# Attention with normed queries and keys: token-major heads replaced by feature-major heads, and its first pair's preparation moved into the last mixture pair

## The reference, cut to what matters

```python
x = x + _L0_ffn_ref(_layernorm(x), ...)                    # mixture of 8 experts, top 2
x = x + _L1_xattn_ref(_layernorm(x), ctx_1024, _lenS2, ...)  # the attention of this document

def _L1_xattn_ref(q, kv, x_seqlens, Wq, Wk, Wv, Wo, q_norm_w, k_norm_w):   # 16 heads of 64
    def rms_norm(x, w):
        return x * jax.lax.rsqrt(jnp.mean(jnp.square(x), -1, keepdims=True) + 1e-5) * w
    qh = rms_norm(heads(q @ Wq), q_norm_w)
    kh = rms_norm(heads(kv @ Wk), k_norm_w)
    vh = heads(kv @ Wv)
    scores = jnp.where(mask, einsum('bhld,bhsd->bhls', qh, kh) / 8, -1e9)
    return einsum('bhls,bhsd->bhld', softmax(scores), vh) @ Wo
```

## Time and profile before

| what | us |
|---|---|
| median of 3 runs | 1215.52 (1208.99 to 1219.18) |
| the profiled execution | 1212.19 |
| its span in the trace | 1210.4 |
| PE busy | 1013.4 |
| DVE busy | 857.5 |
| ACT busy | 573.5 |
| POOL busy | 221.5 |

### The profile page before, as it was taken

The page is one execution under the profiler, slowest core; times in us unless marked ns, Lnnn a source line. Parts: engine busy times, 40 slices in busy tenths (PEclk is TensorE's granted clock), DMA queues, the critical chain, the costliest instruction groups (busy, mean ns, idle before and its releaser), DMA issues.

```text
span 1210.4 us, 32163 instructions
## 1 busy us (share of the span) xinstructions
PE 1013.4 (84%) x11942; PEld 802.7 (66%) x11942; DVE 857.5 (71%) x1921; ACT 573.5 (47%) x1102; POOL 221.5 (18%) x243
## 2 busy tenths in 40 slices
PE   5679999888888887899899999899998673698757
PEld 5448888556656666778678877677877552376535
DVE  5576776789999996555677676677677387576647
ACT  1224443657666663343555565546665231344324
POOL 4563221101111101331100000000000122434200
PEclk9978999989999998999999999999999796599969
DMA  9200000000000000000000000000000000000001
GB/s 371 101 2 1 0 0 0 1 1 2 0 0 0 0 0 2 2 1 1 2 2 0 0 0 2 2 2 0 0 0 1 1 0 0 1 1 0 1 1 35
DMA packets 5921, 16.15 MB, mean 13 GB/s; under 512 B 729, under 2 KB 4962, under 8 KB 5218
## 3 DMA queue, kind: packets, MB, share of 16 engines
q1 hardware_dynamic: 5858, 15.29, 3.3%
HBM read 14.24 MB, written 1.05 MB: 13 GB/s over the span
## 4 chain that ended last, share of the span: by engine, by line
PE 40%; issue 22%; DVE 18%; DVEq 12%; POOL 3%; ACT 2%; POOLq 2%; PEldq 1%; PEld 1%; ACTq 0%
PE banks L1674 7%; PE banks L1747 4%; PE banks L1719 4%; PE banks L900 3%; PE banks L1136 3%; PE banks L1707 3%; DVEq L1346 2%; PE banks L1358 2%; PE banks L1735 2%; PE banks L1117 1%; DVE small L1591 1%; DVE xn L333 1%; DVEq L1012 1%; DVE xr L1011 1%; DVE small L1320 1%
## 5 line engine op out<-in xcount | busy, mean ns | idle before, releaser
L352 POOL TENSOR_TENSOR rstd<-var,nhalf 128x2 f32<-128x2 f32 x72 | 57.3, 796 | 481.2 <-DVE var L326 481.2
L1682 ACT ACTIVATE work<-banks 128x512 f32<-128x512 f32 x128 | 74.9, 600 | 70.6 <-PE banks L1674 70.6
L1339 ACT ACTIVATE work<-work 128x1024 f32<-128x1024 f32 x64 | 67.7, 1057 | 54.9 <-DVEq L1335 31.6
L1674 PE MATMUL banks<-xT_all,weights 128*128 (+1 forms) x384 | 86.2, 380 | 2.3 <-ACT work L1792 1.8
L374 ACT ACTIVATE xT_all<-banks 128x256 f32 (+1 forms) x72 | 28.3, 392 | 120.6 <-PE banks L363 119.6
L1358 PE MATMUL banks<-ident,work 128*128 128x128 f32 x512 | 68.9, 285 | 16.0 <-DVE work L1349 10.9
L929 ACT ACTIVATE work<-banks,weights 128x256 f32<-128x256 f32 x128 | 53.7, 470 | 57.7 <-PE banks L890 56.8
L1674 PEld LDWEIGHTS banks<-xT_all,weights 128*128 128x128 f32 x384 | 71.5, 190 | 13.7 <-ACT work L1792 2.6
L1826 DVE TENSOR_TENSOR work<-banks,neg_mask 128x512 f32<-128x512 f32 x64 | 40.7, 685 | 54.2 <-PE banks L1707 52.6
L1358 PEld LDWEIGHTS banks<-ident,work 128*128 128x128 f32 x512 | 60.9, 147 | 22.8 <-DVE work L1349 13.0
L1747 PEld LDWEIGHTS banks<-weights,work 128*128 128x128 f32 x512 | 58.4, 191 | 14.9 <-ACT work L1792 14.8
(11 more groups left out here) (316 smaller groups left out, 2357.8 us busy)
## 6 DMA issues: line engine op xcount, KB each, us to landing
weights<-wpack SPq DMA_DIRECT2D x1, 5381.5 KB, 32.4
weights<-wpack SPq DMA_DIRECT2D x1, 2060.0 KB, 13.5
weights<-wpack SPq DMA_DIRECT2D x1, 2049.0 KB, 17.9
weights<-wpack SPq DMA_DIRECT2D x1, 1160.5 KB, 20.1
x_all<-x_in SPq DMA_DIRECT2D x2, 512.0 KB, 4.8
ctxT_all<-ctxT_in SPq DMA_DIRECT2D x1, 1024.0 KB, 6.8
out<-x_all SPq DMA_DIRECT2D x8, 128.0 KB, 1.8
rows<-rows_in SPq DMA_DIRECT2D x1, 832.0 KB
```

The lines of the kernel that those rows point to most:

```text
L352: g.tensor_tensor(rstd, var, nhalf[:, 0:2], ALU.pow).then_inc(rstd_ready, 1)
L1339: act.activation(sm[:, u, :], sm[:, u, :], ACT.Exp, scale=scale).then_inc(h["exp"].sem, 1)
L1674: ins = pe.matmul(bank(ring.bank(f"qk{c}"))[:, j * PT:(j + 1) * PT], wt[:, 2 * (c % 4) + j, :], cols(src, p), start=True, stop=True)
L1682: act.activation(dst.rearrange("p c t -> p (c t)"), bank(ring.bank(f"qk{c}")), ACT.Copy) \
```

## The change

**The attention becomes feature-major.** `project` makes queries and keys with the weights as stationary operand, 8 units `qk0` to `qk7` of two 256-column products each, straight from `xT_all` and `ctxT_all`. ACT stores each bank plain and squares the odd ones (in the first pair all); in the bodies POOL squares the even ones from the stored tile. PE sums the squares per head (`sums`: 16 products of 128 rows x 32 columns of the array, 256 wide, in four column groups), ACT takes the inverse root of one 128x256 tile (Ln with scale and bias, Exp), PE spreads the roots times the gains back over the features (`roots_spread`, 16 products of 32 rows, 256 wide, in four row groups, into 8 banks `bc0` to `bc7`), and DVE multiplies each bank into its heads (`scaled`, 8 operations of 128x512). `mean_squares`, `divide`, `turn_qk` and the two stores of turned banks go. The next scores wait for `bc7`.

**The first pair's preparation moves.** `pro` is gone. Its units are spread among those of the mixture's last pair, which is written out behind the loop as `moe0.last`. The mixture's closing sums for its last pair (`add_up`, `ending`) move from ahead of the attention to DVE's place behind the softmax of the first body. The mixture's space in `work` and the attention's are exchanged so that both can be live; ACT's first stores of mixed heads wait for `prod_read`.

**Small things.** `make_gains` on DVE, once, after the first mixture pair. A `settle` ahead of each wait for a bank in the mixture and the attention. The barrier ahead of the attention (all banks empty) goes. POOL copies only `cs` for this attention.

```diff
-        def moe_units(nu, nd, lag):
+        def moe_units(last):
+            early, routed, late = {}, [], []
+            if last:
+                early = {1: ["gains", "qk0", "qk1"], 3: ["qk2", "qk3"], 4: ["qk4", "qk5"], 5: ["qk6", "qk7"],
+                         7: ["sums"]}
+                routed, late = [f"bc{c}" for c in range(4)], [f"bc{c}" for c in range(4, 8)] + [f"v{c}" for c in range(4)]
+            names = ["route"]
+            for j in range(8):
+                names += [f"up{j}"] + early.get(j, [])
+                if j in (3, 5, 7):
+                    names.append(f"down{j // 2 - 1}")
+            names += routed + ["combT", "down3"] + late
...
-        att1 = pipelined(scores4, mixing8, [(f"tok{u}{c}", "a") for u in range(2) for c in range(4)],
-                         values4 + [(f"turn{u}{c}", "av"[c % 2]) for u in range(2) for c in range(4)])
+        att1.pro = moe0.last
+        att1.body = stage(scores4 + queries8 + [("sums", "a")] + turned4 + scaling8[0:4] + mixed4 + scaling8[4:8]
+                          + values4, PAIRS - 1)
+        att1.epi = stage(scores4 + turned4 + mixed4, 1)
...
+            pooled = (0, 2, 4, 6)
...
+            def sums(pe, ring, i, p):
...
+                pe.wait_ge(*ring.emptied(i, "qk7"))
...
+                    pe.wait_ge(*pool_squared.at(p - 1, 1))
...
+                for m in range(4):
+                    for j in range(4):
+                        ins = pe.matmul(bk[32 * j:32 * j + 32, 0:PT], head_sum[:, m, 0, :],
+                                        squares(ring, j // 2)[:, 4 * (j % 2) + m, :], start=(m == 0), stop=(m == 3),
+                                        tile_position=(0, 32 * j))
...
+            def roots_spread(pe, ring, i, p, part):
...
+                        ins = pe.matmul(bank(ring.bank(name))[:, PT * (m % 2):PT * (m % 2) + PT],
+                                        gains_spread[32 * j:32 * j + 32, P * m:P * m + P],
+                                        head_roots[32 * j:32 * j + 32, :], start=True, stop=True,
+                                        tile_position=(32 * j, 0))
...
+                    if last:
+                        result([ring.emptied_before(i, f"o{u}1") for u in range(2)] if ring is s.body else None)
+                    if ring is s.body:
+                        sums(pe, ring, i, p + 1)
+                    probs_turned(pe, ring, i, p, 0, h["prob"])
+                    probs_turned(pe, ring, i, p, 1, h["prob"])
+                    if ring is s.body:
+                        roots_spread(pe, ring, i, p + 1, 0)
...
+                    mix(ring, i, 0)
+                    mix(ring, i, 1)
+                    if ring is s.body:
+                        roots_spread(pe, ring, i, p + 1, 1)
+                        values(pe, ring, i, p + 1)
+                        turn_normed(pe, g_of(s, p), inputs_used)
...
+            def scaled(v, ring, i, k):
+                v.wait_ge(banks_filled, ring.filled(i, f"bc{k}"))
+                v.tensor_tensor(heads_of(k), bank(ring.bank(f"bc{k}")).rearrange("p (c t) -> p c t", t=PT),
+                                heads_of(k), ALU.mult).then_inc(dve_emptied, 1)
...
+                    soft_out(v, p, 0, h)
+                    soft_out(v, p, 1, h)
+                    if last:
                         end[0](v, s, p - 1)
                         end[1](v, s, p - 1)
+                    else:
+                        prog[moe0][6][0](v)
+                        v.drain().then_inc(prod_read, 1)
+                        prog[moe0][6][1](v)
+                    if ring is s.body:
+                        for k in range(8):
+                            scaled(v, ring, i, k)
...
+            def pool(g, p):
...
+                    own = (kT if k else qT)[:, a:a + 2, :]
+                    g.wait_ge(*s.body.emptied(p, f"qk{c}"))
+                    ins = g.tensor_tensor(squares(s.body, k)[:, a:a + 2, :], own, own, ALU.mult)
```

More of the change, by code:

```diff
@@ L215, in stage @@
             return s
-        def pipelined(these, mixing, inputs, late, tail=[]):
-            s = stage([])
-            s.pro = stage(inputs + late, 1)
-            s.body = stage(these + inputs + mixing + late + tail, PAIRS - 1)
-            s.epi = stage(these + mixing + tail, 1)
-            return s
         first = stage([("none", "a")])
@@ new lines, in tensor, with part @@
+                part(s.body, 0, 0)
+                with pe.Fori(1, PAIRS - 1) as p:
+                    part(s.body, p, p)
+                pe.wait_ge(weights_in[weight_group[att1]], 16)
+                part(s.last, 0, PAIRS - 1)
+            def scalar(act):
+                def part(ring, i, p):
+                    for name in ring.names:
+                        if ring is s.last and name == "sums":
+                            act.preload_act_table_set("natural_log_exp_and_others")
+                        if ring is s.last and prog[att1][4][1](act, name):
+                            if name == "sums":
+                                store_turned(act, g_of(s, p), before(act, p))
+                            continue
+                        if not name.startswith("up"):
+                            continue
@@ L1036, in main @@
[L1036 to L1047 removed]
+                    sort(v, ring, i, p)
+                    add_up(v, p - 1)
@@ new lines, in part, with projected @@
+                        result([ring.emptied(i, f"o{u}1") for u in range(2)])
+                steps1(pe, part)
+            def projected(act, ring, i, c):
+                act.wait_ge(banks_filled, ring.filled(i, f"qk{c}"))
+                k, a = c // 4, 2 * (c % 4)
+                bk = bank(ring.bank(f"qk{c}"))
+                ins = act.activation((kT if k else qT)[:, a:a + 2, :].rearrange("p c t -> p (c t)"), bk, ACT.Copy)
+                if ring is s.pro or c not in pooled:
+                    ins = act.activation(squares(ring, k)[:, a:a + 2, :].rearrange("p c t -> p (c t)"), bk, ACT.Square)
+                ins.then_inc(act_emptied, 1)
```

762 lines of the change are left out of this document (369 added, 393 removed).

## The result

| | before | after |
|---|---|---|
| median of 9 runs, us | 1215.47 (1208.99 to 1219.18) | 1204.45 (1201.75 to 1212.92) |
| profiled execution, us | 1212.19 | 1208.06 |
| its span, us | 1210.4 | 1206.3 |

The sign is right and the time is in the range, but about half of the gain is missing. So the question is where 19.2 us became 11.

A forecast was written before the change was run, and what follows sets the result against it. DVE's own order in a chain alternating with PE was taken to bound the attention; -16.8 - 6.9 + 3.5 + 1.0 = -19.2 us gave 1193.0 from the profiled 1212.2, forecast 1195 for the median, range 1185 to 1213.

The forecast's parts named there:

- The six bodies: Normed attention's loop: period 26.7 us instead of 29.5, 16.8 us less over six passes; bounds 25.9 and 29.5.
- The three short waits: PE in a loop body, waiting for banks that DVE must free: 0.1 to 0.3 us each.
- POOL's squares: Loop bodies: POOL and DVE in each other's way add 0.4 us a period; bounds 0 and 3.3.
- the layout: One loop body laid out from its scores at 0, short waits included: ends at 26.3 us, before 0.4 for POOL.
- The last mixture pair: With `pro` in it, router to first scores takes 33.3 us instead of 40.2, 6.9 less; bounds 32.2 and 40.2.
- The first body: Attention's first body, with the mixture's closing sums on its path: 31.5 us against 28.0, 3.5 more; bounds +1.5 and +5.
- `make_gains`: Seven small DVE operations once, between the first two mixture pairs: 1.0 us more, between 0 and 2.9.
- The sum: Whole kernel: -16.8 - 6.9 + 3.5 + 1.0 = -19.2 us, 1193.0 from the profiled execution; median put at 1195.
- `epi` and all later stages keep their code, 0: Stages from `epi` on: same code, so no change in time, 0 us.
- POOL and DVE: Rival: in the attention they hold each other up or the chain stays as long; 1213.1 us, no change; chance 0.12.
- column groups without overlap: Rival: `sums` costs 7.0 us instead of 2.2 in seven bodies and the last mixture pair; 1231.4 us; chance 0.07.
- an empty last mixture pair: Rival: the last mixture pair gains nothing, its 36 units hanging on a ring of six banks; 1199.9 us; chance 0.07.

The follow-up runs named there:

- whole_after: The changed kernel run again without an edit, on another chip, for a second trace: 1205.22 us, ratio 0.9906.
- after_38_ahead: The changed kernel with 38 semaphore increments put at the head of PE's program: 1200.17 us, ratio 0.9861.

## Why the prediction was right where it was, and where it failed

- *The six bodies* (26.7 a period, -16.8): right. The steady period is 26.47, the first of the six passes takes 27.2 and the last 27.4, together 160.5 us for 176.5, so -16.0. By its own rows the forecast's six passes of 26.7 would have saved 16.3, since 176.5 is less than six times the 29.5 that the sum used. PE bounds them, as laid out. `sums` and the two spreads came at 1.94 and 2 x 1.15, for 2.2 each. The three short waits of PE are there, 0.17, 0.36 and 0.57; the last shows as issue.
- *POOL's squares* (+0.4 a period): the mechanism is right, its price on the period isn't measured. The squares don't run at 1.04 us each beside DVE but at 1.56 in the median, and in most passes one of DVE's two subtractions is held, 1.48 for 1.23, which is gone in the run without POOL's squares. That is 0.25 us of DVE's time. The steady period lies 0.17 above the 26.3 of the layout, and the run without POOL can't tell what of it is POOL's, since ACT was late in it. The forecast took DVE's loss beside POOL from `divide` at 5.03 against the softmax's operations; `pro`'s own `divide`, with nothing on POOL beside it, takes 4.63 in the trace of before, so that row said 0.4 and not 0.1. Timeline of DVE in the third pass, and POOL's durations (min/median/max):

```profile
332.60 1.23 DVE L1313 TENSOR_TENSOR work<-work,small 128x1024 f32<-128x1024 f32 x1
...
335.12 1.22 DVE L1311 TENSOR_REDUCE small<-work 128x16 f32<-128x1024 f32 x1
336.41 1.48 DVE L1313 TENSOR_TENSOR work<-work,small 128x1024 f32<-128x1024 f32 x1
```

```profile
L1693 POOL TENSOR_TENSOR weights<-work x28: 1036/1556/2024, 247.4 to 419.1; 128x512 f32<-128x512 f32 x28
...
who waited for it (us, times):
  PE banks L1448: 3.3, 1
```

  In the loop nobody waits for them; the run without them was slower. By the Trainium skill ("SBUF — State Buffer", section "SBUF: two separate sides"), among DVE's operations those with two SBUF inputs contend with a POOL operation that reads SBUF; the page names those in a two-port mode as well, which the prediction left out. The subtraction (L1313) was held, the reductions (1.20 to 1.22) were not, and the trace agrees.
- *The last mixture pair* (33.3): right, 33.67. The wait for `combT` is 0.77 where 1.1 was said, and the granted clock is 1.00.
- *The first body* (31.5): 31.68 in this trace, 30.9 to 31.0 in the other three of after. The wait of 4.20 was named; it is 2.8 in the three others, where `sums` and the transposes behind it ran slower (2.49 and 3.04 us for 1.94 and 1.97 in `whole_after`). Not named was that `sums` waits 3.32 us for POOL, because this body has no `result` to lie between; with the squares on ACT it waits 3.95 for ACT instead. It costs nothing, since PE would only have waited the longer for DVE's scaling. The total is right in this trace by two errors that cancel: the records behind the wait cost 2.4 us more than at the full clock (mix 1.99 for 1.16, spread 2.09 for 1.15, values 4.35 for 3.71), where 1.5 was added, and without that the body takes 29.3 where 30.0 was laid out.
- *`make_gains`* (+1.0): the mixture's seven pairs before the last took 119.4 us instead of 118.7, so +0.7, which is luck. The second pass, where the gains are made, is 0.6 longer than the steady ones. Each of the six passes behind the first is 0.15 longer than before, because PE waits 0.63 us for one of DVE's banks instead of 0.49; the forecast had nothing for that. And the first pass is 0.8 shorter.
- *The sum*: the changed stages gave 18.1 and 18.4 us for 19.2. The agreement at `epi` needs the 1.1 us of the first stage, which is luck. From its own sum the forecast should have said 1193.0 + 3.3 = 1196.3 for the median and not 1195.
- *"`epi` and all later stages keep their code, 0"*: this is the step that failed. The term was put at nothing because the code is the same. In the two traces of each whole kernel (before 755.7 and 762.0 us, after 770.9 and 767.1) the stages from `epi`'s scores on cost 10.1 us more after, of a gain of 19.4; the medians lose some 8. Of the 10.1, 5.6 lie in the plain attentions, where PE stops more often and where the places of the stops move with idle instructions. 1.6 lie in `epi` (granted clock 0.76 instead of 0.83) and the second mixture. The second mixture takes 97.8 to 98.0 us in five traces of before, shifted ones included, 98.5 to 98.7 in six of after's and 99.8 in `after_38_ahead`; why stays open. The rest is in the last blocks, where the same kernel differs by 7.5 us from one trace to the next, so that nothing can be said of them.
- The rivals: POOL and DVE, column groups without overlap and an empty last mixture pair are all out by the trace. None of them was what happened. The missing rival was that the later stages give some of it back.

Theory three (chance) fell for the plain attentions with the repeats. Theory two (a worse hand-over) has the 1.6 us ahead of them for it, but can't explain stops at fixed records in passes that run once, next to steady passes that are equal to the tenth. Theory one stands for the places: they depend on how much code lies ahead, in both kernels and for 38 and 474 instructions, and the change moved them by 54 to 57 records in all three mixes. Its price is less firm. It rests on the comparison of before's places with after's (5.5 us in the means), and at the same places the same stop is 0.25 us long in one trace, 1.45 in another and missing in a third. That before's code at after's places would lose those 5.5 us is argued and not shown.

## What to carry to other kernels

Add the changed stage up from its own rows; that can be right to a microsecond. Then give the unchanged stages a spread of their own instead of nought, those ahead of the change too: here the first stage took 75.4 to 78.8 us with the same code, and the plain attentions 378.0 to 386.4. Before an edit worth 1% is judged, run it once more with some idle instructions ahead, and compare distances inside the changed stages, not only the totals.

## What the runs showed of the hardware

- PE stops where code runs for the first time, for up to 1.9 us at a time, waiting for nothing that the profile shows. In the plain attentions the stops are at the same records in all traces with the same code for PE; their lengths vary (0.73, 0.73 and 0.46 us at one record), and some don't come in each execution. 38 semaphore increments at the program's head move them by 17 to 19 records towards the front, 474 by 19 towards the back. The steady passes (21.7 us, in all traces of both kernels) have none of 0.3 us or more.
- A stop can be followed by records at the low clock level: 128 of the mix in 3.93 us with a granted clock of 0.50 around them, instead of 2.7, in one trace, and not in another behind the same stop.
- A semaphore increment on PE costs 0.156 us on average when 474 stand in a row at the program's head (first product at 73.86 us, all of it "issue"). In the mixture's loop, where one was added ahead of each wait for a bank, 16 records of `up` take 3.70 us with and without it.
- 32 records with 32 columns of the array and 256 wide, in four column groups, take 1.94 us, 0.061 a record, where a record of the whole array of that width takes 0.22.
